# A two-layer graph network on one core: layer 1 without block registers, with its visit sums kept in DRAM and its hot matrices made on ScalarE

## The reference, cut to what matters

```python
x = (feature @ W).reshape(n, H, C)                  # 6250 x 4 x 64
a_src, a_dst = einsum(x, att_src), einsum(x, att_dst)      # 6250 x 4 each
e = leaky_relu(a_src[src] + a_dst[dst], 0.2)        # per edge and head, own loop added
ex = exp(e - segment_max(e, dst)[dst])
alpha = ex / segment_sum(ex, dst)[dst]
out = segment_sum(x[src] * alpha[:, :, None], dst)  # 6250 x 256
h = elu(batch_norm(out + bias))                     # statistics over all nodes
return feature + h
```

## Time and profile before

| | us |
|---|---|
| median of 3 runs | 6006.75 (6001.89 to 6008.48) |
| the profiled execution, its own time | 6008.67 |
| its span, first to last instruction | 6007.0 |
| first gather of `attend_layer1` starts | 4401.05 |
| its last gather starts | 5762.37 |
| last `add` starts | 5799.31 |
| busy over the whole span: TensorE, VectorE, ScalarE, GpSimd | 3490.1, 3201.2, 1444.7, 2239.5 |

### The profile page before, as it was taken

How to read it: one execution, slowest core, us unless ns; L and a number is a source line. 1 busy time by engine, 2 the same in 40 slices (tenths; PEclk the granted TensorE clock), 3 DMA queues, 4 the chain that set the end, 5 groups by cost and what they waited for, 6 DMA issues and landing times. The chain is left out here.

```text
span 6007.0 us, 69289 instructions
## 1 busy us (share of the span) xinstructions
PE 3490.1 (58%) x14745; PEld 2509.9 (42%) x14746; DVE 3201.2 (53%) x6148; ACT 1444.7 (24%) x3456; POOL 2239.5 (37%) x2146
## 2 busy tenths in 40 slices
PE   0499999544444444300017776866657667677753
PEld 0377777332332333200015554541435555555542
DVE  5321122344444444499989997235335555565566
ACT  0122222222222222100003333323223322232312
POOL 0000000455565565300003332003148888778730
PEclk9999999766666666655559999985557777777776
DMA  2322222677777777600016664000123333333321
GB/s 67 101 89 94 94 94 94 207 238 245 249 249 247 247 248 247 191 0 0 0 59 202 201 199 136 0 1 0 32 69 89 90 90 90 90 88 90 93 75 49
DMA packets 490083, 712.91 MB, mean 119 GB/s; under 512 B 62212, under 2 KB 403072, under 8 KB 489646
## 3 DMA queue, kind: packets, MB, share of 16 engines
q0 software_dynamic: 113344, 350.65, 19.9%
q1 hardware_dynamic: 376615, 360.85, 18.3%
HBM read 498.31 MB, written 214.21 MB: 119 GB/s over the span
## 5 line engine op out<-in xcount | busy, mean ns | idle before, releaser
L1534 POOL DMA_INDIRECT g_rows<-x1t,srci x880 | 1057.5, 1202 | 313.0 <-issue 255.8
L762 POOL DMA_INDIRECT rows<-kv,kvi x880 | 834.3, 948 | 597.3 <-DVEq L858 332.9
L846 DVE TENSOR_TENSOR prod<-rows,psD 128x256 f32<-128x256 f32 x880 | 367.6, 418 | 773.6 <-PE psD L805 333.4
L805 PE MATMUL psD<-qs,hot 128*128 x1760 | 617.1, 488 | 250.9 <-issue 154.0
L1663 PE MATMUL g_psM<-g_rows,g_hot 128*128 128x264 f32 x1760 | 584.3, 489 | 102.0 <-DVE g_rows L1783 55.1
L1044 POOL TENSOR_TENSOR wv<-vrows,wgt 128x1024 f32<-128x1024 f32 x110 | 218.8, 1989 | 996.0 <-DMA vrows<-val_v 650.7
L805 PEld LDWEIGHTS psD<-qs,hot 128*128 128x128 f32 x1760 | 386.2, 243 | 433.8 <-issue 380.6
L1120 PE MATMUL psM<-wv,vhot 128*128 128x260 f32 x1760 | 445.3, 396 | 134.3 <-DVE run L1139 127.4
L1663 PEld LDWEIGHTS g_psM<-g_rows,g_hot 128*128 128x128 f32 x1760 | 410.5, 245 | 219.0 <-issue 131.6
L825 ACT ACTIVATE off<-psB,npiota 128x256 f32<-128x256 f32 x440 | 207.9, 472 | 983.0 <-PE psB L796 761.4
L796 PE MATMUL psB<-drrow,identb 110*128 110x256 bf16 x440 | 138.2, 340 | 504.5 <-issue 504.5
(11 more groups left out here) (328 smaller groups left out, 6137.4 us busy)
## 6 DMA issues: line engine op xcount, KB each, us to landing
val_v<-rows SPq DMA_DIRECT2D x220, 512.0 KB
vrows<-val_v SPq DMA_DIRECT2D x220, 512.0 KB
kv<-stage SPq DMA_DIRECT2D x98, 768.0 KB
rows<-kv,kvi POOLq DMA_INDIRECT x880
g_rows<-x1t,srci POOLq DMA_INDIRECT x880
x1t<-pout SPq DMA_DIRECT2D x49, 130.0 KB
fxw<-x1t SPq DMA_DIRECT2D x7, 896.0 KB
xs<-in_x SPq DMA_DIRECT2D x1, 6144.0 KB
```

What stands on the lines that cost most here:

```text
L762: nc.gpsimd.indirect_dma_start(out=rows[:, k], out_offset=None, in_=table, in_offset=bass.IndirectOffsetOnAxis(ap=index[:, i * SLOTS + k:i ...
L805: nc.tensor.matmul(psD[:, k % 4, 0:cols], hot[:, t % 2, j * P:(j + 1) * P], node[:, ds(blk[t], 1)].rearrange("p o d -> p (o d)"), start=Tr ...
L846: ins = nc.vector.tensor_tensor(prod[:, k % 4], rows[:, k, 0:D], psD[:, k % 4, 0:D], ALU.mult)
L1534: nc.gpsimd.indirect_dma_start(out=rows[:, i % NBUF, k, 0:ROW1], out_offset=None, in_=dr["x1t"], in_offset=bass.IndirectOffsetOnAxis(ap=v[ ...
```

## The change

The change removes the registers from TensorE and VectorE in layer 1 and moves work between engines:

- `project_layer1` splits `node` into three bfloat16 parts whose sum is the float32 value, and writes them to DRAM as `nodeb` (48 bytes per node). `prepare_edges` also writes the destinations to DRAM (`drow`, bfloat16) and makes `v["last"]`, the row in DRAM of the last visit of each block.
- In `attend_layer1` the SP queue loads, for each chunk, the destinations broadcast to all partitions (`drow`, 128 x 4096 bytes) and the 8 visits' `nodeb` blocks, with the block numbers in registers of SP. `spread` and `places` go; VectorE makes `g_hotT` in one comparison of 128x2048 bfloat16 (`places_of_nodes`); `expand` becomes 16 bfloat16 matmuls of 24 columns; VectorE reduces the three parts out of PSUM (in `scores`), so ScalarE's copy L1568 goes.
- ScalarE makes `g_hot` (`places_of_edges`: 16 Abs of 128x128 and 4 Relu of 128x512 per chunk) in place of VectorE's L1779.
- ScalarE writes the weights a second time into PSUM (`psW`), and `weigh` multiplies `g_rows` by them from there.
- `add` no longer adds to `acc`: it keeps a running sum, `run[t] = run[t-1] * same[V] + psM`, over the 8 visits of a chunk, with four `g_psM` banks, and SP saves all of them to DRAM (`sums`, two DMAs of 540672 bytes per chunk). `finish` fetches the last visit of each block with 49 indirect DMAs on GpSimd and does the division by groups of seven blocks as they land.
- The order: `weigh(i+1, 0)` and `own_weights(i+1)` stand at the end of iteration i, behind `scores(i+2)`; `add` 6 and 7 slip into the next iteration; TensorE does the softmax steps of chunk i+1 in groups 0, 1 and 2 and `expand(i+2)` there too, and only `scatter` in group 3.

```diff
@@ prepare_edges
+                sp.dma_start(dr["drow"].rearrange("(i t s) -> i t s", t=VT, s=SUP), v["drrow"][0:NT]).then_inc(s_wr, 16)
...
+                step(tsc(lastf[:, 0:NB - 1], psum[:, 3, 0:NB - 1], 1.0, float(P), ALU.subtract, ALU.mult))
+                step(nc.vector.memset(lastf[:, NB - 1:NB], float((NV - 1) * P)))
+                step(tsc(v["last"][:], lastf[:], c["piota"][:, 0:1], None, ALU.add))
@@ project_layer1
+                step(nc.vector.tensor_copy(part[:, :, 0], node[:]))
+                step(nc.vector.tensor_tensor(left[:], node[:], part[:, :, 0], ALU.subtract))
+                step(nc.vector.tensor_copy(part[:, :, 1], left[:]))
+                step(nc.vector.tensor_tensor(left[:], left[:], part[:, :, 1], ALU.subtract))
+                nc.vector.tensor_copy(part[:, :, 2], left[:]).then_inc(part_done, 1)
...
+                sp.wait_ge(part_done, 1)
+                sp.dma_start(dr["nodeb"].rearrange("b p d -> p b d"), part[:].rearrange("p b s n -> p b (s n)")).then_inc(kept, 16)
@@ attend_layer1, SP
+                def nodes(i):
+                    if i >= 2:
+                        sp.wait_ge(dst_done, NGRP * (i - 1))
+                    sp.dma_start(drow[:, i % 2], dst[i].to_broadcast([P, CH * P])).then_inc(nd_in[i % 2], 16)
+                    for u in range(2):
+                        sp.load(regs, v["blk"][0:1, CV * i + 4 * u:CV * i + 4 * u + 4])
+                        for k in range(4):
+                            at = sp.snap(regs[k], min_val=0, max_val=NB - 1)
+                            sp.dma_start(ndt[:, i % 2, 4 * u + k], dr["nodeb"][ds(at, 1)].rearrange("o p d -> (o p) d")).then_inc(nd_in[i % 2], 16)
+                def save(i, u):
+                    sp.wait_ge(run_done, CV * i + 4 * (u + 1))
+                    sp.dma_start(sums[2 * i + u], run[:, 4 * u:4 * u + 4]).then_inc(saved[u], 16)
...  (per iteration: save(i, 0); nodes(i + 4); row_flags(i + 3), as before; save(i, 1))
@@ ScalarE
+                def places_of_edges(i, g):
+                    n = NGRP * i + g
+                    for k in range(GRP):
+                        K = i * CH + g * GRP + k
+                        ins = nc.scalar.activation(far[:, n % 2, k], c["iota"][:], ACT.Abs, scale=-1.0, bias=v["dr"][:, K:K + 1])
...
+                    if i:
+                        act.wait_ge(sum_done, CV * (i - 1) + 2 * g + 2)
...
+                    nc.scalar.activation(hot[:, g * GRP:(g + 1) * GRP], far[:, n % 2], ACT.Relu, bias=1.0, scale=-1.0).then_inc(hot_done, 1)
@@ weights
+                        act.wait_ge(wv_done, NGRP * i)
+                    nc.scalar.activation(psW[:, 0:HT].rearrange("p (t h) -> p t h", h=H), dl[:, :, 0:H], ACT.Exp).then_inc(wt_done, 1)
                 for i in range(-2, NCH):
+                    if chunk(i):
+                        places_of_edges(i, 3)
                     if chunk(i + 1):
+                        places_of_edges(i + 1, 0)
+                        entering(i + 1)
+                        places_of_edges(i + 1, 1)
                         weights(i + 1)
+                        places_of_edges(i + 1, 2)
@@ TensorE
-                def spread(i, g):
...
                 def expand(i, g):
+                    if g == 0:
+                        pe.wait_ge(nd_in[i % 2], 16 * (CV + 1) * (i // 2 + 1))
+                        pe.wait_ge(hotT_done, i + 1)
+                        if i:
+                            pe.wait_ge(col, 3 * i - 2)
+                    for k in range(GRP * g, GRP * (g + 1)):
+                        ins = nc.tensor.matmul(psD[:, k].rearrange("p s n -> p (s n)"), hotT[:, i % 2, k * P:(k + 1) * P], ndt[:, i % 2, k // 2],
+                                               start=True, stop=True)
+                    ins.then_inc(dst_done, 1)
...
                     for g in range(NGRP):
                         if chunk(i):
                             scatter(i, g)
+                        if chunk(i + 2) and g < 3:
+                            expand(i + 2, g)
+                            if g == 2:
+                                expand(i + 2, 3)
+                        if chunk(i + 1):
+                            (row_ends, carry_back, top_back, skip)[g](i + 1)
@@ VectorE
+                def places_of_nodes(i):
...
+                    tsc(hotT[:, i % 2], drow[:, i % 2], c["piota"][:, 0:1], None, ALU.is_equal).then_inc(hotT_done, 1)
+                    nc.vector.tensor_reduce(e[:, i % 2], psD[:].rearrange("p t s n -> p t n s"), AX.X, ALU.add).then_inc(col, 1)
                 def weigh(i, g):
-                    tt(hot[:, k], c["iota"][:].unsqueeze(1).to_broadcast([P, GRP, P]), ...
-                    tt(out, out, rows[:, b, k, D:ROW1].unsqueeze(3).to_broadcast([P, GRP, H, DK]), ALU.mult).then_inc(wv_done, 1)
+                    dve.wait_ge(wt_done, i + 1)
+                    w = psW[:, g * GRP * H:(g + 1) * GRP * H].rearrange("p (t h) -> p t h", h=H)
+                    tt(out, out, w.unsqueeze(3).to_broadcast([P, GRP, H, DK]), ALU.mult).then_inc(wv_done, 1)
                 def add(i, t):
...
+                    if i and t % 4 == 0:
+                        dve.wait_ge(saved[t // 4], 16 * i)
+                    before = run[:, t - 1] if t else base[:]
+                    stt(out=run[:, t], in0=before, scalar=v["same"][:, V:V + 1], in1=psM[:, V % 4, 0:MSG], op0=ALU.mult, op1=ALU.add).then_inc(run_done, 1)
```

```diff
@@ finish
+        acc = sb("facc", [P, NB, MSG])
+            @block.gpsimd
+            def _(pool):
+                for b in range(NB):
+                    nc.gpsimd.indirect_dma_start(
+                        out=acc[:, b], out_offset=None, in_=dr["sums"],
+                        in_offset=bass.IndirectOffsetOnAxis(ap=v["last"][:, b:b + 1], axis=0)).then_inc(acc_in[b // G7], 16)
-                with dve.Fori(0, NG7) as b:
+                for b in range(NG7):
+                    k = slice(b * G7, (b + 1) * G7)
+                    own, dn, zr = acc[:, k, D + H:MSG], den[:, k], zero[:, k]
+                    dve.wait_ge(acc_in[b], 16 * G7)
+                    step(tt(dn, acc[:, k, D:D + H], own, ALU.add))
...  (the six steps of L1927 to L1932, now for seven blocks at a time)
```

232 lines of the change are left out of this document (108 added, 124 removed).

## The result

The kernel after takes 5967.64 us (median of 4 runs, 5962.82 to 5973.84) against 6004.32 us for the kernel before (4 runs, 6001.18 to 6008.48) measured beside it: ratio 0.9939, 95% interval 0.9922 to 0.9956. The forecast was 5828 and at most 5910. It is faster, by 0.6% and not by 3%. The profiled execution took 5962.82 us, with a span of 5961.1.

What follows compares the result with a forecast made beforehand. Layer 1's attention was taken as bound by gathers end to end on POOL. Terms -223 + 27 - 18 + 0 + 10 + 24 + 1 = -179 gave 5828 us; likeliest range 5780 to 5875, low 5775, up to 5910.

Steps and rivals of the forecast that it cites:

- The chain through one chunk: Layer 1 attention: from one set of scores to the next, 15 to 18.5 us, at most 20, below the gathers' 20.6.
- Rival (b): Layer 1 attention: the dependent steps of a chunk become the bound at 22 us per chunk; 5909 us, chance 0.12.
- POOL's 34.5 us in excess: Layer 1 attention: POOL's idle time against PE, about 37 us with small ones; 19 taken as left, so -18 us.
- Weighing: Layer 1 attention: with weights in PSUM and the one-hot off DVE, gathers keep 949 ns; -223 us, the main term.
- The comparison 128x2048: New DVE operation once per layer 1 chunk, about 0.63 us; may stop gathers, +27 us, bounds nothing or 35.
- First gather: project_layer1, before the attention gathers: five more operations and a DMA of short runs, +10 us, bounds +6 and +30.
- Tail: End of layer 1 attention, last gather's end to last sum's end, 36.4 us before: no change, bounds -6 and +6.
- `finish`: Final stage: 49 gathers held up by DVE's two-input operations, about 12 us per group; +24 us, bounds +10 and +51.
- rival (d): finish: its gathers run freely beside DVE's two-input passes, 9.6 us per period, +10 not +24; 5814 us, chance 0.10.
- (a): Layer 1 attention: gathers still stand still in the weighing, so the 223 us stay; +44, 6051 us, chance 0.07.
- (c): Layer 1 attention: the SP or ACT queue becomes the bound; at 25 us per chunk 6074 us, chance 0.04.

Runs made afterwards that it cites:

- e16: The kernel after, unchanged, measured again beside the kernel before on a chip in the undisturbed condition: 5494.25 us against 5678.94, ratio 0.9672.
- e17: The kernel after with the sums kept in SBUF, no saves and no gathers in finish, run undisturbed: ratio 0.9615 to the kernel before.
- e3: The kernel after with node rows loaded for the first two chunks only and reused by all others: ratio 0.9915 to the kernel before.

## Why the prediction was wrong, point by point

**The step that failed** is "The chain through one chunk": "15 us at the higher clock, 18.5 at the lower, with handovers up to 20; all below 20.6". It took for granted that an engine hears of TensorE's end at once. In the disturbed condition a handover from TensorE cost 3.4 us in the median and over 9 in a tenth of the cases, and the pace was 23.1 us where 20.6 was forecast. Rival (b) named the place, a chain of 22 us or more, but for other reasons (clock and single buffers) and with too little; 5910 as the upper end left no room for it. The sign of it stood in the rows: POOL's 34.5 us in excess "against PE", which I took as 37 us that may or may not return. They were most likely the same stalls, rare there because the weighing kept interrupting the gathers: the wait before the fourth chunk, 22.7 us in the kernel before, is 12.2 in the kernel after disturbed and 0.3 undisturbed. I forecast 19 us of the 37 to be left; it became 175 (136.5 + 68.2, less 0.3 for each of the 98). The trace of the kernel before held a second sign, in the unchanged layer 0: the 304.2 us for which L846 waited on "remote". The same line in e16 waits for TensorE by name and never on "remote".

**The rest, in the disturbed profile.** Weighing: -223 forecast, -214.6 of gather time in total with all else in it. The comparison 128x2048: 759 ns, not 0.63 us. It does hold gathers up: it runs beside 21 of the 24 gathers over 1.05 us (all of 33 undisturbed). But such a gather loses 0.3 to 0.4 us and not the whole comparison, so the excess is 9 us (10) against 27, a term that was mis-sized. First gather +6.8 us (+10); from layer 0's last gather to it the stretch grew by 12.0 us (1925.5 against 1913.5), and layer 0 happened to be 5 us shorter. Tail from the end of the last gather to that of the last sum 29.7 us against 36.4, -6.8, just past the bound of -6. `finish`: the end of the seventh bias addition is 100.0 us after the last sum against 70.0, +30 where I had +24, with this rhythm of a group:

```profile
5789.96 0.19 DVE L1999 TENSOR_TENSOR fden<-facc 128x28 f32<-128x28 f32 x1 [2.62 <-DMA facc<-sums_v,lastvisit]
...
5791.42 2.02 DVE L2011 TENSOR_TENSOR ft<-fxw,fzero 128x1792 f32<-128x1792 f32 x1
...
5802.29 0.19 DVE L1999 TENSOR_TENSOR fden<-facc 128x28 f32<-128x28 f32 x1 [2.56 <-DMA facc<-sums_v,lastvisit]
```

12.3 us, forecast 12; rival (d) is out. With the stage's -75.3 this makes +6.8 - 75.3 - 6.8 + 30.0 - 0.6 (all that follows) = -45.9, which is the difference of the spans.

**Undisturbed** the sum holds: -184.7 us against -179, a pace of 20.3 against 20.6, gathers of 962 ns. The chain is shorter than worked out, 13.8 us, and VectorE idles 6.5 us per chunk where I had 2 to 5. Saves and `finish` together, less what the registers on VectorE cost, come to 34.8 us (e16 less e17), more than the 20 to 25 expected. There is no undisturbed trace of the kernel before, so its terms can only be estimated: of the 325 us between its two conditions, 301 would be layer 0's (1402.3 us less 1101.4), which leaves some 24 for its attention stage, then 1337 us long; the stage's change would then be -224 against -223 + 27 - 18 = -214. That the sum came out within 6 us is in part luck: by this estimate a stage shorter by 10 us than forecast and a tail shorter by 7 stand against a `finish` dearer by 6 and a first gather 4 later.

**Rivals.** (a) is out: free gathers in both conditions. (c) is out: e3, with nearly nothing on SyncE but flags and saves, gains nothing, and undisturbed the same queues of SyncE and ScalarE carry 20.3 us a chunk. A version that beats both kernels is e17, sums in SBUF: 0.9615 against 0.9672 for the kernel after, undisturbed; it wasn't run disturbed.

## What to carry to other kernels

When several engines wake in the same instant from waits on one engine whose work is recorded as long begun, the loss may be in the report of completion and not in the work; look how often it happens before you sum up durations, and price a small unexplained gap by what it would be if it came every round. A loop of the two engines alone shows it in one run. And before a gain is judged small, measure it once more later, with the kernel before beside it, and compare the lengths of stages that the change leaves alone: here the same change was worth 0.6% and 3.3%, and the missing events in the trace and an unchanged layer 0 of 1398.5 and 1101.4 us told the two apart.

## What the runs showed of the hardware that I had not expected

- A VectorE product of 1.2 us with one input in SBUF and one in PSUM leaves GpSimd's indirect gathers alone (955 to 977 ns in the mean, over all versions with the weights in PSUM and full rows), one with both in SBUF holds them up (1082 with the product alone, 1178 with the comparison too, 1202 before).
- Beside free gathers, in the disturbed condition, each TensorE instruction took 1.40 us in a loop, for as long as 27 us after the last gather; plain loads of the same rows did nothing of the kind.
- The disturbed condition cost the kernel before 5.7 to 6.9% and the kernel after 8.6% (5967.64 against 5494.25). By the stages of the kernel after, all of it lies in the two stages with rows of gathers.
